# A cross-attention kernel: the value product two Gram passes earlier, and VectorE's fold ahead of the deviation

## The reference

```
q = Wq y + bq      k = Wk y + bk      v = Wv x + bv
scores = q k^T / sqrt(128)     in 8 heads of 16 channels, summed over the 1024 positions
attn   = softmax(scores)
o      = Wo (attn v) + bo + x
out    = (o - mean(o)) / sqrt(var(o) + 1e-5) * gn_w + gn_b     mean and var over the whole batch
```

## Time and profile before

| what | us |
|---|---|
| median of the runs | 168.95 |
| the profiled execution's own time | 167.54 |
| its span, first to last instruction | 165.6 |
| PE busy | 155.0 (94%) |
| PEld busy | 121.8 (74%) |
| DVE busy | 150.7 (91%) |
| ACT busy | 138.9 (84%) |
| POOL busy | 98.3 (59%) |

### The profile page before, as it was taken

How to read it: one execution, slowest core, us unless ns; L and a number is a source line. 1 busy time by engine, 2 the same in 40 slices (tenths; PEclk the granted TensorE clock), 3 DMA queues, 4 the chain that set the end, 5 groups by cost and what they waited for, 6 DMA issues and landing times. The chain is left out here.

```text
span 165.6 us, 3745 instructions
## 1 busy us (share of the span) xinstructions
PE 155.0 (94%) x932; PEld 121.8 (74%) x932; DVE 150.7 (91%) x686; ACT 138.9 (84%) x354; POOL 98.3 (59%) x162
## 2 busy tenths in 40 slices
PE   7998999999999999999999999999999999999720
PEld 7896888777777788877777778888777777886400
DVE  1788999999999999999999999999999999987661
ACT  3784599999999999999999989999999999977441
POOL 3049366777666676667766667666776666651110
PEclk9999999999999999999999999999999999999996
DMA  5999769999999999999999999999999987732333
GB/s 187 410 417 410 291 223 287 334 330 333 354 381 298 303 350 364 352 345 346 344 351 313 366 340 340 340 336 334 334 356 377 364 311 262 251 130 101 124 145 139
DMA packets 14276, 50.82 MB, mean 307 GB/s; under 512 B 1712, under 2 KB 1712, under 8 KB 14256
## 3 DMA queue, kind: packets, MB, share of 16 engines
q1 hardware_dynamic: 13824, 50.08, 83.4%
q10 hardware_dynamic: 432, 0.53, 0.9%
HBM read 33.82 MB, written 16.78 MB: 305 GB/s over the span
## 5 line engine op out<-in xcount | busy, mean ns | idle before, releaser
L666 PE MATMUL o_ps<-x_sb,m_sb 128*128 128x512 f32 x124 | 60.8, 613 | 0.0
L666 PE MATMUL g_ps<-hl_sb 128*128 128x258 f32 x256 | 46.4, 304 | 0.0
L456 DVE TENSOR_TENSOR hl_sb<-y_sb,hl_sb 128x512 fp32r<-128x512 f32 x64 | 44.0, 692 | 0.0
L325 ACT CAST hl_sb<-y_sb 128x512 fp32r<-128x512 f32 x64 | 40.0, 629 | 2.1 <-DMA y_sb<-in_ctx_dram 2.0
L546 DVE BATCH_NORM_STATS2 bn<-o_ps 128x6 f32<-128x512 f32 x62 | 40.3, 687 | 1.6 <-PE o_ps L666 1.6
L404 ACT ACTIVATE out_sb<-o_ps,shift,gain 128x1024 f32<-128x1024 f32 x31 | 37.5, 1210 | 0.1
L252 POOL TENSOR_TENSOR lsuma<-hl_sb 128x256 f32<-128x256 f32 x30 | 21.9, 731 | 25.3 <-DVE hl_sb L456 25.3
L666 PEld LDWEIGHTS g_ps<-hl_sb 128*128 128x128 f32 x256 | 35.0, 191 | 0.2 <-DVE hl_sb L456 0.2
L263 POOL TENSOR_TENSOR lsumb<-hl_sb 128x256 f32<-128x256 f32 x30 | 21.9, 729 | 18.1 <-DVE hl_sb L456 18.1
L666 PEld LDWEIGHTS o_ps<-x_sb,m_sb 128*128 128x128 f32 x124 | 21.2, 191 | 14.8 <-issue 14.8
L274 POOL TENSOR_TENSOR lsum<-lsuma,lsumb 128x256 f32<-128x256 f32 x30 | 22.4, 747 | 4.2 <-issue 0.4
(11 more groups left out here) (76 smaller groups left out, 287.8 us busy)
## 6 DMA issues: line engine op xcount, KB each, us to landing
y_sb<-in_ctx_dram SPq DMA_DIRECT2D x32, 512.0 KB, 6.1
x_sb<-in_x_dram SPq DMA_DIRECT2D x32, 512.0 KB, 6.9
out_dram<-out_sb SPq DMA_DIRECT2D x31, 512.0 KB, 6.0
w_in<-in_weights_dram ACTq DMA_DIRECT2D x1, 256.0 KB, 5.6
out_dram<-out_sb ACTq DMA_DIRECT2D x1, 256.0 KB, 2.6
out_dram<-out_sb SPq DMA_DIRECT2D x1, 256.0 KB, 2.8
cols<-in_columns_dram ACTq DMA_DIRECT2D x1, 3.0 KB, 3.5
```

Of the source, the lines that this page charges most:

```text
L325: nc.scalar.copy(hl_sb[:, b % SLOTS, chunks, 0:C], y_sb[:, b % SLOTS, chunks, :]).then_inc(h_ready, 1)
L456: nc.vector.tensor_tensor(hl_sb[:, b % SLOTS, chunks, C:2 * C], y_sb[:, b % SLOTS, chunks, :], hl_sb[:, b % SLOTS, chunks, 0:C].bitcast(F3 ...
L666: return nc.tensor.matmul(dst, lhsT, rhs, start=start, stop=stop, **more)
```

## The change

Two orders are changed, and no instruction is added or taken away. In TensorE's list the eight Gram passes are cut into 2, 2 and 4 in place of 4 and 4, and the value product stands behind the first two. In VectorE's list the fold (with the addition of bo that belongs to it) stands between aggregate and deviation, and the pivot ahead of the square.

```diff
@@ VectorE's list
                 aggregate(t - 4)
+                fold_matrix(t - 3)
                 deviation(t - 4)
-                fold_matrix(t - 3)
+                pivot_column(t - 3)
                 square(t - 4)
-                pivot_column(t - 3)
                 rest_half(t, 0)
@@ gram
-            def gram(b, half):
+            def gram(b, chunks):
...
-                pe.wait_ge(l_ready, 2 * b + 1 + half)
-                if half == 0 and b >= 1:
+                pe.wait_ge(l_ready, 2 * b + (1 if chunks[-1] < HCH else 2))
+                if chunks[0] == 0 and b >= 1:
...
-                for c in range(half * HCH, (half + 1) * HCH):
+                for c in chunks:
@@ TensorE's list
                 query(t - 2)
-                gram(t - 1, 0)
+                gram(t - 1, range(0, 2))
                 value_product(t - 3)
-                gram(t - 1, 1)
+                gram(t - 1, range(2, HCH))
+                gram(t - 1, range(HCH, CH))
                 scores(t - 2)
```

More of the change, by code:

```diff
@@ L682, in gram @@
                         pe.wait_ge(s_copied, b)
-                for c in range(half * HCH, (half + 1) * HCH):
+                for c in chunks:
                     mm = product(g_ps[:, 0:HL], hl_sb[:, b % SLOTS, c, 0:C], hl_sb[:, b % SLOTS, c, :],
                                  start=(c == 0), stop=(c == CH - 1))
-                if half == 1:
+                if chunks[-1] == CH - 1:
                     mm.then_inc(hl_ready, 1)
@@ L773, in _ @@
                     diag[:, :, :].rearrange("p v e -> p (v e)")).then_inc(rows_ready, 1)
-            gram(0, 0)
-            gram(0, 1)
+            gram(0, range(0, HCH))
+            gram(0, range(HCH, CH))
             low_sum(0, range(0, HCH))
@@ L781, in _ @@
             query(0)
-            gram(1, 0)
-            gram(1, 1)
+            gram(1, range(0, HCH))
+            gram(1, range(HCH, CH))
             scores(0)
@@ L787, in _ @@
             query(1)
-            gram(2, 0)
+            gram(2, range(0, HCH))
             softmax_product(0)
-            gram(2, 1)
+            gram(2, range(HCH, CH))
             value_product(0)
```

## The result

The changed kernel took **170.66 us** (median of six runs, 170.34 to 170.73) beside 168.31 us (six runs, 167.82 to 169.55) for the kernel before in the same comparison. The ratio is **1.0133**, with a 95% interval from 1.0101 to 1.0166: slower, and by more than 1%. 170.6 us was predicted, inside a range of 168.6 to 172.3. But the kernel before was at 168.31 here and not at 168.95, so the change cost 2.2 us (0.0133 x 168.31) where 1.7 were forecast, and a part of the loss has another cause than the one I gave.

The account below looks back on a forecast made before the run. A loop through ScalarE and TensorE was taken to bound the kernel at 4.57 us a pass, becoming 4.62 set by TensorE. 1.35 + 0.28 + 0.12 - 0.07 = 1.68, so 168.95 + 1.7 = 170.6 us, range 168.6 to 172.3.

Parts of the forecast that it names:

- output loop: Closed loop through ScalarE (copy of r to copy of the cross part) and TensorE (transpose to softmax product), said to set 4.57 us a pass.
- new wait of 0.17 us: TensorE's load for the value product, now behind two Gram passes, would wait 0.17 us for ScalarE's copy of r.
- hole of 0.10: Predicted sign: about 0.10 us without any load shown, in front of TensorE's load of r for the value product.
- six Gram loads in a row: Predicted sign: TensorE's six remaining Gram loads follow one another behind the value product.
- transpose without a wait: TensorE would reach the transpose's load at 111.12, after ScalarE's copy allows it (111.08), so its old 0.03 us wait goes.
- fold's earlier start: Predicted sign: VectorE's fold starts 0.07 us earlier against the softmax product.
- rival by which the wait would be absorbed: Rival, chance 0.22: TensorE's loads have room, so the wait at the value product costs nothing; time 168.95 us.
- Fold, bo, deviation and square see no other wait: Step on VectorE's new order: these four run without further waits, the square ending at 110.71.
- statistics' wait: TensorE's 0.08 us wait before the statistics' load, forecast to go with cover 0.07; waiting behind the square would prove the prediction wrong.
- statistics rival: Rival, chance 0.13: the square ends later than 110.78, the 0.11 us of TensorE waits is not given back; 173.6 us.
- VectorE as the bound: Rival, chance 0.05: VectorE's instructions end to end set the period; the new order saves 0.12 us a pass; 165.5 us.
- disturbed pass: One pass where VectorE's deviation took 0.37 us rather than 0.16; the forecast took 0.07 us off for it.

## Why the prediction was right where it was, and where it wasn't

**The output loop as the bound before: right, but only just.** Shortening ScalarE's part of it gained 0.36%, and the value product's move by one pass, which leaves it alone, gained nothing. But it added up to 4.57 beside a second loop, through VectorE and POOL, of 4.55 to 4.56, which the prediction doesn't have. One reading inside the sum is off without changing it: TensorE's row has the input product's first matmul at 111.32, 0.03 and not 0.11 behind its load, and its four passes take 1.80 to the softmax product at 113.12.

**The new wait of 0.17 us: right,** in the rows (0.16 to 0.17) and by itself: TensorE's half alone has 4.636 us a pass, and the forecast was 4.62 with a few longer passes. The hole of 0.10, the six Gram loads in a row, the transpose without a wait and the fold's earlier start are as forecast. The rival by which the wait would be absorbed is refuted, and with it what I had drawn for this case from the Trainium skill's page "Perfetto Trace Analysis", section "Identifying the Most-Contended Engine": the loads were busy for 104.02 us of 132 before and for 102.21 after, and the time went up. The room in the mean was not where the wait was.

**The price of VectorE's half: wrong.** The step that failed is "Fold, bo, deviation and square see no other wait". I looked for what each instruction waits for, and not for what runs beside it: moving the deviation behind the fold took it from the end of POOL's second add, too late to be held by it, to the beginning of the last one. The median pass shows it at 0.42 us. The consequences were three. The statistics' wait did not vanish but kept 0.04 of its 0.08, the prediction's own sign of being wrong. The passes are 4.67 apart and not 4.62. And the sum put nothing down for VectorE's half, where that half alone costs 2.8 us (0.0167 x 168.11), more than the whole forecast.

**The sum: close by luck.** The one cost in it is real, the other was put at nothing, and the two compete instead of adding up. Of 2.2 us by the ratio, TensorE's wait accounts for 1.2 to 1.6 (TensorE's half, and the whole change with the one-input deviation, 0.0074 and 0.0093 of 168.11), and the hold adds the remaining 0.7 to 1.0. Each of these ratios is known to 0.3%, or 0.5 us; the passes tell it more sharply, 28 x 0.061 = 1.7 of 28 x 0.093 = 2.6 us for the wait and 0.9 for the hold. Had the two added up instead, it would have been 4.

**The statistics rival** ("the square ends later through a slower chain deviation, pivot, square", 0.13) named the right place, with the wrong size: the wait kept 0.04 of its 0.08 us, and not the 0.11 of both waits. It had the chain slower in itself, where it is one instruction held by another engine. **VectorE as the bound** was refuted in its form: the time didn't fall. But VectorE was in a loop only 0.01 to 0.02 us below the bound, and with the hold on the deviation it is in the one that counts. "VectorE waits there", ahead of the fold, was true and hid that: behind the fold it waited for POOL.

**Two readings of the old trace** were wrong. I entered the long deviation of the disturbed pass as chance, and took 0.07 off for it; the earlier trace rows with POOL's row beside it shows the mechanism. And in the ordinary pass of the earlier trace rows I took the square's 0.26 for spread, "as long as 0.26 rather than 0.21", with the pivot 0.18 behind it where I reckoned with 0.13. POOL's row beside it shows that this was the same hold. What delayed POOL in the disturbed pass is open, but it isn't chance: the same idle of 0.42 or 0.43 us stands ahead of the same add once in every one of the twelve traces, between 95 and 98 us in eleven, and at 144 us in the kernel in which POOL has one instruction more per pass.

**The forecast's own range** of 0.9 to 2.6 us counts 29 passes and the two end passes again; with 27 it is 0.9 to 2.5. That changes no reading.

## What to carry to other kernels

Before an instruction of one engine is moved in its list, put the rows of the engines it shares something with beside it, at the old and at the new place. A one-column operation of VectorE with two inputs in SBUF can last until the end of the GpSimd add that it falls into; written with one of them as a scalar it doesn't. What counts is then how much VectorE still has to do behind the release before it feeds GpSimd again: 0.06 us with the pivot alone, 0.20 with pivot and square. And a product moved ahead in TensorE's list is free only until its load meets the end of the copy that it reads, so that the distance (here one Gram pass, not two) is read from those two rows.

A record that is longer than its like, in one pass or in all, is worth a look at what ended at the same instant on every other engine: it may be the price of the change.

## What the runs showed of the hardware

- A VectorE instruction of one column with two tensor inputs in SBUF that starts within one of GpSimd's adds ends 0.01 to 0.02 us behind that one's end: 102.80 and 102.78, 96.37 and 96.36, 103.21 and 103.19, 102.75 and 102.73, 103.03 and 103.01, 110.57 and 110.56. As a tensor_scalar with one SBUF tensor the deviation keeps its 0.20 us; the fold and the addition of bo, with one operand in PSUM, keep their 0.29 and 0.15.
- Not every GpSimd instruction does this: a rest of 128x512 with two SBUF inputs takes its 0.68 us although it starts within a GpSimd power of one column that lasts 0.55.
- Perhaps the hold goes the other way too (one case, not tested): GpSimd's add of 64 columns took 0.83 us in place of 0.32 when it started 0.02 behind such a rest.
- GpSimd's add of 128 columns takes 0.46 us, and two adds of 64 take 0.60 together, at 0.32 each: splitting one costs 0.14.
- The loop through VectorE and GpSimd sets VectorE's pace from the start: in the changed kernel the rests behind the square are 4.67 to 4.69 apart from the first passes on, the disturbed pass apart. TensorE keeps its own 4.62 to 4.63 for four passes, in which the deviation begins earlier and earlier within the add (0.27 us long in the second pass, 0.41 in the fifth), and then waits for VectorE at 4.67.
